# Convolution stage of a four-layer graph network: TensorE's turn of h moves to the first place of a slot, behind the turn of x3

## The reference

```
# layer 2: X_k = adj^k x for k = 1..3, for both of its (equal) adjacencies
parts = [x, chebyshev(adj, x, 3), chebyshev(adj, x, 3)]
y2 = einsum('bnik,iok->bno', concat(parts), weight_1)
x = layernorm(x + y2)
# layer 3
features = relu(x @ psi_w + psi_b)
messages = (adj * adj).T @ features
h = relu(concat(messages, x) @ phi1_w + phi1_b)
x = layernorm(x + h @ phi2_w + phi2_b)
```

## Time and profile before

| what | value |
|---|---|
| median of 3 runs | 1387.19 us (1386.95 to 1387.49) |
| the profiled execution's own time | 1387.39 us |
| its span in the trace | 1385.2 us |
| busy: TensorE matmul, weight load | 1349.8 us (97%), 1184.3 us (85%) |
| busy: VectorE, ScalarE, GpSimd | 1108.6 us (80%), 927.9 us (67%), 753.7 us (54%) |
| convolution stage, all its slots | from about 951 us (first turn of h, woven in) to the end of the span |

### The profile page before, as it was taken

The page is one execution under the profiler, slowest core; times in us unless marked ns, Lnnn a source line. Parts: engine busy times, 40 slices in busy tenths (PEclk is TensorE's granted clock), DMA queues, the critical chain, the costliest instruction groups (busy, mean ns, idle before and its releaser), DMA issues.

```text
span 1385.2 us, 26908 instructions
## 1 busy us (share of the span) xinstructions
PE 1349.8 (97%) x8470; PEld 1184.3 (85%) x8470; DVE 1108.6 (80%) x2632; ACT 927.9 (67%) x1666; POOL 753.7 (54%) x745
## 2 busy tenths in 40 slices
PE   9999979999999999999999999999889999999995
PEld 7888868888888888888888888887689999999994
DVE  5888878777778777778777787777688888888885
ACT  5666647677777776777777777766546666666664
POOL 4111127666666666666666666665435555555553
PEclk9999999999999999999999999999999999999998
DMA  3222232000021000020000110000212222222211
GB/s 107 96 92 91 96 103 77 1 0 0 9 82 32 0 0 0 30 83 8 0 0 0 46 46 1 0 0 8 76 54 70 70 68 68 68 68 68 68 39 38
DMA packets 60041, 61.16 MB, mean 44 GB/s; under 512 B 4691, under 2 KB 39381, under 8 KB 59989
## 3 DMA queue, kind: packets, MB, share of 16 engines
q1 hardware_dynamic: 59556, 60.31, 13.6%
q10 hardware_dynamic: 432, 0.20, 0.1%
HBM read 35.33 MB, written 25.17 MB: 44 GB/s over the span
## 4 chain that ended last, share of the span: by engine, by line
PE 94%; DVE 3%; ACT 2%; issue 1%; POOL 0%; ACTq 0%; POOLq 0%; DVEq 0%
PE psum L969 6%; PE psum L663 5%; PE psum L665 5%; PE psum L651 5%; PE psum L346 4%; PE psum L365 4%; PE psum L981 3%; PE psum L983 3%; PE psum L706 3%; PE psum L695 3%; PE psum L678 3%; PE psum L707 3%; PE psum L676 3%; PE psum L696 3%; PE psum L699 3%; PE psum L698 3%
## 5 line engine op out<-in xcount | busy, mean ns | idle before, releaser
L626 POOL TENSOR_TENSOR rh_lo<-rh,rh_hi 128x512 fp32r<-128x512 f32 x160 | 207.1, 1294 | 265.6 <-ACT rh_hi L741 265.6
L632 POOL TENSOR_TENSOR h_lo<-h,h_hi 128x512 fp32r<-128x512 f32 x160 | 216.6, 1354 | 12.8
L741 ACT CAST rh_hi<-rh 128x512 fp32r<-128x512 f32 x160 | 99.4, 621 | 149.2 <-DVE rh L773 149.2
L754 DVE TENSOR_TENSOR psum<-psum,h 128x512 f32<-128x512 f32 x160 | 111.9, 699 | 103.5 <-ACT psum L745 103.5
L663 PE MATMUL psum<-adj_t_hi,hn_hi 128*128 128x256 f32 x640 | 172.1, 303 | 1.0 <-DVE m_lo L767 1.0
L738 ACT ACTIVATE psum<-psum,bias_cols 128x512 f32<-128x512 f32 x160 | 106.8, 667 | 80.1 <-PE psum L683 80.0
L665 PE MATMUL psum<-adj_t_hi,hn_lo 128*128 128x256 f32 x640 | 158.9, 282 | 0.0
L773 DVE TENSOR_TENSOR rh<-psum,h 128x512 f32<-128x512 f32 x160 | 110.1, 688 | 50.3 <-ACT psum L738 50.2
L663 PEld LDWEIGHTS psum<-adj_t_hi,hn_hi 128*128 128x128 f32 x640 | 121.8, 190 | 1.9 <-issue 1.8
L665 PEld LDWEIGHTS psum<-adj_t_hi,hn_lo 128*128 128x128 f32 x640 | 122.2, 191 | 0.0
L728 ACT ACTIVATE z<-psum,bias_cols 128x512 f32<-128x512 f32 x160 | 111.3, 695 | 0.0
(11 more groups left out here) (184 smaller groups left out, 4119.8 us busy)
## 6 DMA issues: line engine op xcount, KB each, us to landing
x_in<-in_x_dram SPq DMA_DIRECT2D x32, 256.0 KB, 2.8
x_dram<-x SPq DMA_DIRECT2D x32, 256.0 KB, 2.1
g_x<-x_dram SPq DMA_DIRECT2D x32, 256.0 KB, 3.3
h_dram<-h SPq DMA_DIRECT2D x32, 256.0 KB, 2.0
ht<-h_dram SPq DMA_DIRECT2D x32, 256.0 KB, 2.9
c_x<-x_dram SPq DMA_DIRECT2D x32, 256.0 KB, 3.1
out_dram<-res SPq DMA_DIRECT2D x32, 256.0 KB, 2.4
conv_in<-in_L_gnn_weight_dram SPq DMA_DIRECT2D x1, 448.0 KB, 4.8
```

The lines of the kernel that those rows point to most:

```text
L626: pool.tensor_tensor(rh_lo[:, q, :], rh[:, q, :], rh_hi[:, q, :].bitcast(F32), ALU.subtract).then_inc(rh_lo_done, 1)
L632: pool.tensor_tensor(h_lo[:, q, :], h[:, (g - 1) % G, :], h_hi[:, q, :].bitcast(F32), ALU.subtract).then_inc(h_lo_done, 1)
L754: dve.tensor_tensor(cb, cb, hg, ALU.subtract).then_inc(dif_done, 1)
```

## The change

The block of the turn of h moves, as it stands, from behind the layer 3 features to the front of TensorE's slot. The turn of x3 is the last step of the slot before, so the two turns now stand next to each other; the first weights and the features come behind them. No instruction is added or removed, and no other engine's program is touched.

```
@@ -988,6 +988,16 @@
             s = it * U + u
             w, wq = s - L_W, (u - L_W) % 2
             m = s - L_F
+            if live(it, u, 0):
+
+                pe.wait_ge(y1_loaded[u % 2], it * (32 * U // 2) + 32 * (u // 2 + 1))
+                wait_count(pe, y1_done, s)
+                if isinstance(it, int) and s == 2:
+                    pe.wait_ge(x2t_lo_done, 1)
+                for b in range(GB):
+                    for c in range(KC):
+                        mm = pe.transpose(psum[:, B_T1, cols(tile(b, c))], ht[:, u % 2, cols(b * KC + c)], ident[:, :])
+                mm.then_inc(y1_mm, 1)
             if live(it, u, L_W):
 
                 pe.wait_ge(x2t_lo_done, w + 1)
@@ -1010,16 +1020,6 @@
                     mm = pe.matmul(psum[:, B_F, cols(i)], x3t[:, cols(i)], psi[:, :],
                                    start=False, stop=True, skip_group_check=True)
                 mm.then_inc(f_mm, 1)
-            if live(it, u, 0):
-
-                pe.wait_ge(y1_loaded[u % 2], it * (32 * U // 2) + 32 * (u // 2 + 1))
-                wait_count(pe, y1_done, s)
-                if isinstance(it, int) and s == 2:
-                    pe.wait_ge(x2t_lo_done, 1)
-                for b in range(GB):
-                    for c in range(KC):
-                        mm = pe.transpose(psum[:, B_T1, cols(tile(b, c))], ht[:, u % 2, cols(b * KC + c)], ident[:, :])
-                mm.then_inc(y1_mm, 1)
             if live(it, u, L_W):
 
                 wait_count(pe, y2_done, w)
```

## The result

The changed kernel takes 1398.59 us (median of 6, 1396.89 to 1401.47) against 1387.22 for the kernel before in the same comparison: a ratio of 1.0085 with a 95% interval of 1.0071 to 1.0099, slower by 9.8 to 13.7 us. The forecast was 1400.0, in the range 1395.8 to 1404.3.

A forecast was written before the change was run, and what follows sets the result against it. The prediction took a chain through ScalarE and VectorE from f_mm to spread 1, balanced with TensorE's work, as the bound. 28 x 0.44 + 0.44 = 12.8 us gave 1400.0 us, range 1395.8 to 1404.3.

The forecast's parts named there:

- What bounds it: f_mm to spread 1: a chain f_hi, f_lo, c_y, statistics, c_lo of level 1 takes 3.51 us, balanced with TensorE's work.
- Slot 32: Slot without turn of h or c_y: features to spread 1 takes 4.48 us against 4.56, taken to show the chain limits.
- The turn, 0.44 us: Slot start to f_mm: the turn of h, now ahead of f_mm, adds 0.44 us a slot (ends 0.42 and 0.60).
- From spread 1 to the slot's end: Last stretch of TensorE's slot: nothing moves against each other, so 0 us.
- Two waits of 0.44 us together: f_mm to spread 1: messages about 0.06 us late, spread 1 waits some 0.4 us for c_lo; gain 0.
- VectorE's wait before f_lo would grow from 0.37 to about 0.8: Expected trace sign on VectorE: its idle time before f_lo rises from 0.37 us to about 0.8.
- the question whether spread 0 is late: Spread 0 against c_lo of level 0, whose source w_mm moves with f_mm: reached 0.14 us behind it, so not late.
- Slot 2 +0.44, slot 3 nothing: Early slots: slot 2 pays 0.44 us (bounds 0 and 0.9) through c_lo of level 0; slot 3 pays 0.
- The sum, 12.8: Whole kernel: 28 x 0.44 + 0.44 = 12.8 us slower, 1400.0 us for the median, +0.9%.
- the place doesn't matter: Rival: TensorE's work is unchanged and the chain could be 3.07 us, so not slower, 1385.5 to 1387.2 us; chance 0.08.
- The clock: Rival: new waits beside the transposes lower TensorE's granted clock, 1.7 us lost a slot, 1448 us; chance 0.02.
- The late load: Rival: loads landing after 5.0 us stall the turn at the front, 0.5 us a slot, 14 us more, 1414; chance 0.03.

The follow-up runs named there:

- e1: Changed kernel with the turn of h done twice, in the new place and again in the old one; 1397.19 us, ratio 1.0085.
- e10: Kernel before with the turn of h done twice in its old place; 1395.43 us, ratio 1.0070.
- e6: Changed kernel with c_y's statistics behind c_lo of level 1 and ScalarE's res split around c_hi of level 1; 1389.76 us, ratio 1.0026.
- e8: Changed kernel with ScalarE's res split and c_y's statistics split, two before and two behind c_lo of level 1; 1386.64 us, ratio 1.0006.
- e2: Changed kernel with the turn of h moved behind the first weights, still ahead of the features; 1398.44 us, ratio 1.0100.
- e5: Changed kernel with ScalarE's res split, two of four pieces behind c_hi of level 1; 1398.42 us, ratio 1.0082.
- e4: Changed kernel with VectorE's statistics of c_y moved behind c_lo of level 1; 1403.22 us, ratio 1.0117.
- e7: Kernel before with VectorE's statistics of c_y moved behind c_lo of level 1; 1395.91 us, ratio 1.0071.
- e9: Kernel before with three of c_y's four statistics before c_lo of level 1 and the last behind it; 1384.95 us, ratio 0.9992.

## Why the prediction was right

**What bounds it.** Right. The stretch from f_mm to spread 1 is 3.50 to 3.51 us in all 28 slots of the changed kernel, and e1, e10, e6 and e8 show that the chain, and not the work or the place, sets it. Slot 32 was weaker evidence than it was taken for: without c_y, VectorE is idle there for 1.3 us before c_lo, and what holds spread 1 is the other chain, through ScalarE's res (3.42). It showed that a chain over 3.07 us would be left, not that the chain through c_y was the limit.

**The turn, 0.44 us.** Right for its own stretch: from the turn of x3 to f_mm the slot takes 3.66 us, and 3.22 before. From spread 1 to the slot's end, put at 0, it takes 0.02 less (4.63 against 4.65). A slot costs 0.42 in the mean, 11.7 us in 28, which puts the sum 0.6 us high.

**Two waits of 0.44 us together.** Right: the messages start 0.05 us late (load at 1163.81, against a pitch of 0.12 behind 1163.64, the last of spread 0), and spread 1 waits 0.40.

**VectorE's wait before f_lo would grow from 0.37 to about 0.8.** Wrong: in slot 16 it stayed 0.37, in most others it went from 0.41 to 0.44. The added idle stands one step earlier, 0.53 us in front of c_lo of level 0, because w_mm is late by the turn too. I had used that for the question whether spread 0 is late and forgot it here. e2, where w_mm is early, shows 0.81. It changes no term of the sum.

**Slot 2 +0.44, slot 3 nothing.** Spread 0 of the two slots in the changed kernel:

```profile
999.13 0.38 PE L981 MATMUL psum<-c_hi,adj_t_hi 128*128 128x256 f32 x1 [0.69 <-DVE c_lo L1159]
...
1009.90 0.39 PE L981 MATMUL psum<-c_hi,adj_t_hi 128*128 128x256 f32 x1 [1.76 <-DVE c_lo L1159]
```

They are 1.25 and 1.24 us later than before, so slot 3 added nothing. Of the 1.25, 0.95 were there when TensorE reached slot 2 (995.42 against 994.47), in work that the change does not touch (0.85 by the end of the gated layer): one profiled execution against another. Slot 2 itself added 0.30.

**The sum, 12.8.** From the parts as measured: 11.7 + 0.3 = 12.0, and with those 0.95 it is the 12.9 by which the spans differ. The medians differ by 11.4, and the interval of the ratio, 9.8 to 13.7, holds 12.0. The forecast was at the high side by a little over 1 us, which single runs of the changed kernel (1396.9 to 1401.5) spread over anyway. The stated range, 1395.8 to 1404.3, is not the one that the terms were added up to (1396.7 to 1404.9), and its ends are not derived; the result lies in both.

**The rivals.** That the place doesn't matter needed c_lo to end within 3.07 us of f_mm: so only once two other engines had been reordered (2.97 in e6, 3.07 in e8). The clock did not fall with the new waits: from 1010 to 1350 us of the changed kernel it was 1.00. The argument about it was thin, though. In the kernel before the 0.83 is made of 3 us at 0.50, from 992 to 995, behind a wait of 1.76 us that ended at 991.85; the wait of the same length in slot 3 had no such sequel. These rows don't say what makes the difference, and 0.83 was no measure for waits of 0.4 us. The late load came once, in e5, and not in the changed kernel.

## What to carry to other kernels

When an engine is full and never seems to wait, measure from the step that it releases to the step that it needs back. If a chain through the other engines is just as long, work moved from behind the release to ahead of it is paid in full; once it has been moved, as much work again behind the release is free, as in e1. The price of a place lies in what is released late, and the repair in shortening every chain that ends there, not the first one found. When a step is moved to fill or open a gap, look at what stood in that gap: it was covering a wait for somebody else.

## What the runs showed that was not expected

A step of the slot that waits for the instruction directly ahead of it on its own engine can show an idle time that it did not have before. With a statistic directly ahead of the step that adds up the statistics, VectorE is idle for 0.22 us between the two in the first slot of each loop pass, and for 0.03 in the three others, in e4, e6, e7, e8 and e9; with c_lo between them, as in the kernel before, for 0.00. Slot 16, of which many rows here are, is such a first slot, and in e6 and e7 its wait at L1056 is the long one: a single slot of a loop is not the mean of its loop.

A wait of a weight load is not its price. In most slots of e6 the load at L1056 waits 0.32 us, but from spread 1 to the next turn of x3 the slot takes 4.81 us instead of 4.65: 0.16 was paid. The load starts 0.51 us behind the one before it, where without the wait it is 0.23, so it is 0.28 late. The next load then follows after 0.13 instead of 0.23, and the one behind the turn of x2 after 0.53 instead of 0.56, which gives back the rest.
